# First experts' scores spread through a table in DRAM, groups routed two ahead, zeros written in the first layer

## The reference, cut to what matters

```
logits = x @ gate_w.T;  probs = softmax(logits);  topk_w = top_k(probs, 4) / its sum
scores = topk_w spread over 16 columns (0 for the experts not chosen)      # [tokens, 16]
g, u = x @ w1[e], x @ w3[e]                                                # 16 experts, 64 hidden features
out  = sum over e of ( silu(g) * u  @ w2[e] ) * scores[:, e]
```

## Time and profile before

| | us |
|---|---|
| median of three runs | 3887.02 |
| the profiled execution | 3887.59 |
| its span (first to last instruction) | 3885.8 |
| of which layer 0's experts, from its first load to the next stage | 674.9 to 1111.3 |

### The profile page before, as it was taken

One profiled execution on the slowest core, in us unless ns is written; L12 is line 12 of the kernel. 1 busy time (PEld: TensorE's weight loads), 2 busy tenths in 40 slices (PEclk: granted clock), 3 DMA queues, 4 the chain that ended last, 5 costly groups with the idle time before them and its releaser, 6 DMA issues. The chain is left out here.

```text
span 3885.8 us, 78038 instructions
## 1 busy us (share of the span) xinstructions
PE 2962.6 (76%) x23501; PEld 1869.2 (48%) x23501; DVE 3009.3 (77%) x12214; ACT 2259.2 (58%) x4496; POOL 1882.8 (48%) x2125
## 2 busy tenths in 40 slices
PE   3777776899979999699399967886777677677357
PEld 1222222444447777354277655554555555555245
DVE  6999998566667787343688867886999999999456
ACT  4999998333336666243266645664666666666230
POOL 5777776000013656577344452223236666666661
PEclk9999999999989999799699989998566766666585
DMA  2000000850000000153300000000001110000037
GB/s 76 5 5 5 5 5 19 374 250 1 1 14 14 27 28 27 46 142 114 97 15 15 15 13 1 2 2 12 12 25 50 33 31 7 5 5 4 1 101 228
DMA packets 161160, 177.79 MB, mean 46 GB/s; under 512 B 71906, under 2 KB 136324, under 8 KB 153323
## 3 DMA queue, kind: packets, MB, share of 16 engines
q1 hardware_dynamic: 128108, 140.65, 11.7%
q0 software_dynamic: 23424, 27.94, 2.1%
q10 hardware_dynamic: 9216, 4.20, 0.4%
HBM read 80.48 MB, written 113.61 MB: 50 GB/s over the span
## 5 line engine op out<-in xcount | busy, mean ns | idle before, releaser
L405 PE MATMUL PS<-IDENT,a_T 128*77 128x128 f32 (+1 forms) x3584 | 588.3, 302 | 157.9 <-ACT a_Pr L556 138.6
L1062 ACT ACTIVATE l_H<-l_H 128x2048 f32<-128x2048 f32 (+2 forms) x256 | 597.4, 2711 | 2.9 <-POOL l_H L1114 2.7
L405 PEld LDWEIGHTS PS<-IDENT,a_T 128*77 128x77 f32 (+1 forms) x3584 | 464.2, 164 | 243.3 <-ACT a_Pr L556 105.5
L1114 POOL TENSOR_TENSOR l_H<-l_feat,l_text 128x4096 f32<-128x4096 f32 x64 | 450.4, 7038 | 131.4 <-PE PS L1018 130.7
L1018 PE MATMUL PS<-l_H,l_wide 128*32 128x512 f32 (+1 forms) x2560 | 332.1, 594 | 165.2 <-ACT l_H L1062 165.2
L1136 DVE TENSOR_TENSOR l_H<-PS,l_text 128x2048 f32<-128x2048 f32 (+1 forms) x192 | 411.7, 2146 | 2.1 <-ACT l_text L1089 2.1
L558 ACT ACTIVATE a_Pr<-PS 77x512 f32<-77x512 f32 (+1 forms) x640 | 374.7, 587 | 60.5 <-PE PS L405 60.5
L422 PE MATMUL PS<-a_Pr,a_vaug 77*32 77x128 f32 (+1 forms) x7168 | 306.2, 316 | 23.4 <-ACT a_OT L597 15.8
L659 POOL TENSOR_TENSOR a_T<-a_mx,a_T 128x616 f32<-128x616 f32 x128 | 155.5, 1215 | 292.7 <-DVE a_mx L725 292.7
L2676 POOL DMA_INDIRECT expert_rows<-e3r_row,e3r_rows_at x256 | 253.5, 990 | 89.4 <-issue 74.7
L109 POOL TENSOR_TENSOR RSTD<-norm_tmp,MINUS_HALF 128x24 f32<-128x24 f32 x6 | 25.1, 4189 | 553.2 <-DVE norm_tmp L102 553.2
(11 more groups left out here) (382 smaller groups left out, 7871.6 us busy)
## 6 DMA issues: line engine op xcount, KB each, us to landing
pair_rows<-e_zero SPq DMA_DIRECT2D x35, 1024.0 KB, 25.3
expert_shares<-e_zero SPq DMA_DIRECT2D x16, 1024.0 KB, 25.7
e3c_four<-expert_shares SPq DMA_DIRECT2D x64, 256.0 KB, 3.7
e_xin<-pair_rows SPq DMA_DIRECT2D x39, 264.0 KB, 3.1
e_four<-pair_shares SPq DMA_DIRECT2D x16, 512.0 KB, 4.1
e_w<-in_L_ffn_blocks SPq DMA_DIRECT2D x39, 194.0 KB, 2.5
e3x_xin<-expert_rows SPq DMA_DIRECT2D x32, 200.0 KB
expert_rows<-e_zero SPq DMA_DIRECT2D x6, 1024.0 KB, 24.8
```

The source lines that it names most:

```text
L405: last = pe.transpose(PS[0:keys, 4 + g % 2, j * S:(j + 1) * S], T[:, u, c:c + keys], m.IDENT[:, :])
L1062: act.activation(cells, cells, ACT.Tanh).then_inc(q[f"tanh{part}"], 1)
L1114: pool.tensor_tensor(H[:, a, lo * S:hi * S].rearrange("p (t f) -> p t f", f=S), bcast(feat[:, a, :], 1, hi - lo), bcast(text[:, a, lo:hi], ...
```

## The change

It alters five things.

1. The pick product, its bf16 matrix, its load (`c_pick_pairs`, 288 KB) and cast, the split in three bf16 parts and their four transposes go. VectorE's `route_weights` ends with the fp32 scores; TensorE turns them with one fp32 transpose of 128x64 (`turn_scores`, pair 7, into bank 4), ScalarE copies 64x128 into `scT`.
2. SyncE writes `scT` in four transfers of 8 KB to a table in DRAM (16 experts x 512 tokens, one of two), waits for them, and reads the table back in two transfers of 1 MB: in each, every one of 64 partitions gets the 2 KB rows of the 8 experts that are first (or second) in their pair. The result, `wide` [128, 8 x 512] fp32, two of them, is what `hid` now multiplies with, from SBUF. The read waits for the last `hid` of the group that used the buffer before.
3. Groups are routed two ahead: `turn_y`, logits, the routing and `turn_scores` of step s are of group s+2 (yT in three buffers), `normalise_group` is of group s+3. The first group's products start after two routings and not one.
4. VectorE waits at pair 0 for both reads of its group.
5. The zeroed tile is made by GpSimd in `layer0_cross`' first block, and the 59 zeroing transfers are issued there, one a step after the load of `qm`; SyncE waits for all at that stage's end.

The diff, cut to its core:

```diff
@@ layer0_cross, SyncE's step
+                if i == 0:
+                    sp.wait_ge(m.s_zero, 1)
+                clear_part(sp, m, zero, i)
             run_written_out(sp, step, 0, 0)
+            sp.wait_ge(m.s_cleared, m.cleared)
@@ route_weights
-    dve.tensor_copy(parts[:, :, 0:E], sc).then_inc(q["hi"], 1)
-    dve.tensor_tensor(rest, sc, parts[:, :, 0:E], ALU.subtract).then_inc(q["rest1"], 1)
-    dve.tensor_copy(parts[:, :, E:2 * E], rest).then_inc(q["mid"], 1)
-    dve.tensor_tensor(rest, rest, parts[:, :, E:2 * E], ALU.subtract).then_inc(q["rest2"], 1)
-    dve.tensor_copy(parts[:, :, 2 * E:3 * E], rest).then_inc(q["parts"], 1)
@@ layer0_experts
+        @block.sync
+        def _(sp):
+            for i in range(NG):
+                u = i % 2
+                table = m.scores[u * E:(u + 1) * E, :]
+                sp.wait_ge(q["scTs"], i + 1)
+                if i >= 2:
+                    sp.wait_ge(q[f"wide{u}"], i // 2 * 32)
+                for g in range(G):
+                    sp.dma_start(table[:, g * S:(g + 1) * S], scT[g * E:(g + 1) * E, u, :]).then_inc(q[f"kept{u}"], 16)
+                sp.wait_ge(q[f"kept{u}"], (i // 2 + 1) * (G * 16))
+                if i >= 2:
+                    sp.wait_ge(q["hid"], nth_part(i, NP - 1, NP, 2 * NP))
+                for half in range(2):
+                    sp.dma_start(wide[64 * half:64 * half + 64, u, :].rearrange("f (p n) -> f p n", n=N),
+                                 table.rearrange("(p h) n -> h p n", h=2)[half].partition_broadcast(64)) \
+                        .then_inc(q[f"wide{u}"], 16)
@@ TensorE
-                if p == 0:
-                    pe.wait_ge(q["partsTs"], q.nth("partsTs", i))
-                if past_part(i, p, NP, 1):
-                    pe.wait_ge(q["hid"], nth_part(i, p, NP, 1))
-                pe.matmul(PS[:, 4, :], pick[:, p * 128:(p + 1) * 128], r.partsT[:, u, :],
-                          start=True, stop=True).then_inc(q["up"], 1)
+            def turn_scores(i):
+                pe.wait_ge(q["prob"], i + 1)
+                if i >= 1:
+                    pe.wait_ge(q["scTs"], i)
+                pe.transpose(PS[0:G * E, 4, 0:S], r.sc[:, i % 2, :], m.IDENT[:, :]).then_inc(q["scT"], 1)
-            run_written_out(pe, step, 1, 1, NG)
+            for s in range(-2, NG + 1):
@@ VectorE
+                        if p == 0:
+                            dve.wait_ge(q[f"wide{u}"], (s // 2 + 1) * 32)
-                        dve.tensor_tensor(hid[:, v, :], gu[:, v, :], PS[:, 4, :], ALU.mult).then_inc(q["hid"], 1)
+                        dve.tensor_tensor(hid[:, v, :], gu[:, v, :], wide[:, u, p * N:(p + 1) * N], ALU.mult) \
+                            .then_inc(q["hid"], 1)
```

More of the change, by code:

```diff
@@ L943, in layer0_cross @@
         one = sb("one", [S, 1])
+        zero = sb("zero", [128, 2048])
         q = Signals(ctx, nc, "l0", [
@@ L1227 @@
 N = G * S
-ROWS = 72
 PAD = 8
@@ L1344, in front_tensor @@
[L1344 to L1372, removed]
@@ L1418, in layer0_experts @@
         total = sb("total", [D, 2, N])
-        zero = sb("zero", [128, 2048])
-        q = Signals(ctx, nc, "e0", ROUTE_SIGNALS + ["prep", "up", "silu", "gu", "hid", "down"])
+        q = Signals(ctx, nc, "e0", ROUTE_SIGNALS + ["up", "silu", "gu", "hid", "down", "scT", "scTs", "kept0", "kept1",
+                                                    "wide0", "wide1"])
         PS = m.PS
@@ L1451, in _, with turn_y, logits @@
         @block.tensor
         def _(pe):
-            turn_y, logits, turn_parts = front_tensor(pe, m, q, y, yT, gate, r, E)
-            def up(i, u, p):
+            def turn_y(i):
+                pe.wait_ge(q["y"], i + 1)
+                if i >= 1:
+                    pe.wait_ge(q["yT"], i)
+                for g in range(G):
+                    last = pe.transpose(PS[:, 6, g * S:(g + 1) * S], y[:, i % 2, g * D:(g + 1) * D], m.IDENT[:, :])
+                last.then_inc(q["yTps"], 1)
+            def logits(i):
+                pe.wait_ge(q["yT"], i + 1)
+                if i >= 3:
+                    pe.wait_ge(q["x"], i - 2)
+                for g in range(G):
+                    last = pe.matmul(PS[:, 7, g * E:(g + 1) * E], yT[:, i % 3, g * S:(g + 1) * S], gate[:, :],
+                                     start=True, stop=True)
+                last.then_inc(q["logits"], 1)
@@ L1472, in down @@
             def down(i, p):
                 pe.wait_ge(q["hid"], nth_part(i, p, NP))
-                if p == 0:
-                    if past(i, 1):
-                        pe.wait_ge(q["total"], q.nth("total", i, 1))
-                last = pe.matmul(PS[:, 5, :], w2[:, p, :], hid[:, p % 2, :], start=(p == 0), stop=(p == NP - 1))
-                last.then_inc(q["down"], 1)
-            def turn_total(i, u):
-                pe.wait_ge(q["total"], q.nth("total", i))
-                pe.wait_ge(q["lt"], q.nth("lt", i, -1, NG))
+                if p == 0 and i >= 1:
+                    pe.wait_ge(q["total"], i)
@@ L1483, in turn_total @@
+                pe.matmul(PS[:, 5, :], w2[:, p, :], hid[:, p % 2, :], start=(p == 0), stop=(p == NP - 1)) \
+                    .then_inc(q["down"], 1)
+            def turn_total(i):
+                pe.wait_ge(q["total"], i + 1)
+                pe.wait_ge(q["lt"], min(i + 2, NG - 1) + 1)
                 for g in range(G):
-                    last = pe.transpose(PS[:, 7, g * D:(g + 1) * D], total[:, u, g * S:(g + 1) * S], m.IDENT[:, :])
+                    last = pe.transpose(PS[:, 7, g * D:(g + 1) * D], total[:, i % 2, g * S:(g + 1) * S], m.IDENT[:, :])
@@ L1562, in _ @@
             norm_gpsimd_rest(pool, m)
-            pool.memset(zero[:, :], 0.0).then_inc(m.s_zero, 1)
-        @block.sync
-        def _(sp):
-            clear_rows(sp, m, zero)
 PAIR = 2
@@ L2377, with clear_part @@
 PLACES = B * S * CHOSEN
-def clear_rows(sp, m, zero):
+def clear_part(sp, m, zero, i):
     width = zero.shape[1]
-    sp.wait_ge(m.s_zero, 1)
-    n = 0
     for table in (m.pair_rows, m.rows, m.shares):
         flat = table.rearrange("(p a) d -> p (a d)", p=128)
-        for c in range(0, flat.shape[1], width):
+        parts = -(-flat.shape[1] // width)
+        if i < parts:
+            c = i * width
             part = min(width, flat.shape[1] - c)
             sp.dma_start(flat[:, c:c + part], zero[:, 0:part]).then_inc(m.s_cleared, 16)
-            n += 16
-    m.cleared = n
-    sp.wait_ge(m.s_cleared, n)
+            m.cleared += 16
+            return
+        i -= parts
 def make_router(nc, m, t, ctx, wfT, row, own, rank, hid):
@@ L3245, in laid_out @@
     out["c_width_features"] = width.T
-    row, pair = np.arange(72), np.arange(8)
-    half = 2 * pair[None, :, None] + (f // 64)[None, None, :]
-    out["c_pick_pairs"] = ((row[:, None, None] % 16 == half) & (row[:, None, None] < 48)).astype(np.float32)
     for dh in (8, 16):
```

154 lines of the change are left out of this document (68 added, 86 removed).

## The result

The changed kernel takes **3852.59 us**, the median of four runs (3851.86 to 3856.70), against 3888.80 (3886.40 to 3891.39, four runs) for the kernel before: a ratio of 0.9909, 95% interval 0.9892 to 0.9926, so 0.9% faster, 36 us by the medians. The forecast was 3857.

A forecast was written before the change was run, and what follows sets the result against it. TensorE's own time and its waits were taken to bound layer 0's experts. From 3887.6 us, 40.7 less for the groups and 10.9 more for the opening gave 3857.8, as a median 3857; range 3845 to 3877.

The forecast's parts named there:

- The group: Layer 0's experts: a routed group falls from 25.82 to 23.4 us; over all groups 40.7 us less.
- The stall: TensorE's wait at pair 6 or 7 for ScalarE's two table loads: grows from 0.40 to 0.75 us a group.
- the turn of the scores: One fp32 transpose replaces four bf16 ones on TensorE: 0.17 us for 0.25, 0.08 gained a group.
- Rival B: Ordinary pairs become bound by the chain to hid: 1 us a group, 16 in all, 3873 us; chance 0.14.
- The opening: Start of the experts' stage: first hid 9.9 us late, plus 1.0 for half clock, costing 10.9 us.
- the data time T: Time for a group's 2.1 MB table read, scaled from broadcast row length: 13.1 us at 160 GB/s.
- The clock: TensorE products at half clock after idling in the opening: 1.0 us added, bounds 0 to 3.
- The reads in the steady state: Table reads after group 0 stay hidden up to T about 20 us: no wait, 7 us of cover.
- Rival A: The table reads bound each group, from below 105 GB/s; at 79 GB/s 3985 us; chance 0.10.
- The zeros: Zeroing transfers moved into layer 0's attention: no effect on its time.
- Rival C: The zeroing slows layer 0's attention by 1%: 3863 us; at 5% 3888; chance 0.06.
- D: The stall before the turn at pair 7 stays: 13.6 us back, 3871 us; chance 0.05.

The follow-up runs named there:

- the run without tables: Changed kernel with ScalarE computing 1 + 0.05 x in place of the experts' exponential, so no activation table loads; ratio 0.9892 to the kernel before.
- short rows: Changed kernel with eight reads of 256 KB a group, in pieces of 512 B in place of 2 KB; 3986.6 us beside 4022.9 for the kernel before.
- the routing one ahead: Changed kernel with groups routed one ahead, not two, so reads are issued in the step that uses them; 4220.1 us beside 4038 for the kernel before.
- the transfer with two outermost entries: Kernel with the turn moved, reading a re-laid table in one 2 MB transfer whose outermost dimension is the two halves; 4177.6 us, ratio 1.0741.
- the turn moved: Changed kernel with the turn back of a group's output moved from pair 2 to pair 5, its X addition a step later; 3850.59 us, ratio 0.9892.
- the run of their own: Kernel before with only the 59 zeroing transfers moved to layer 0's attention; ratio 0.9980.
- the split kept: Changed kernel with VectorE's five splitting instructions put back before the turn of the scores, their output unused; ratio 0.9942 to the kernel before.
- the long rows: Kernel with the turn moved, its table re-laid in 16 KB pieces and read by two transfers of 64 partitions; 3854.5 us beside 3892.8 for the kernel before.

## Why the prediction was right, step by step

**The group.** Forecast 23.4, measured 23.21. The pick products' 1.74 and the 0.97 before the turn came as worked out. The stall is 0.63 in the place of 0.75, but the load of w2, for which I had added 0.1, now lengthens the product behind it by 0.10: together 0.33 more than before, where I had 0.35. Its cause was right: the run without tables takes it all away, and the run with a transpose put into it takes 0.45. The term that was mis-sized is the turn of the scores. It holds TensorE 0.11 us (747.30 to 747.41), not 0.17, and the w1 product behind it takes 0.86, where it took 0.92 behind the four transposes (746.32 to 747.24): 0.20 gained and not 0.08. So 25.82 - 1.74 - 0.97 - 0.20 + 0.33 = 23.24. Over the 13 pitches from turn to turn the group gives 2.2 us more than forecast, the first group 0.4 less, the last two 0.1 more: this is the 1.9 between -40.7 and -42.6.

**hid from SBUF and the ordinary pairs.** Nothing was forecast and nothing came: hid takes 0.692 us in the place of 0.686, and without the tables TensorE is busy through all of a group. Rival B, an idle time before down in ordinary pairs, did not come about.

**The block before.** -2.1 forecast, -1.75 measured. I had the first y 0.35 us behind GpSimd's last instruction; it follows the barrier, 1.0 behind it (GpSimd ends at 679.01, y starts at 680.03).

**The opening.** +9.9 forecast for the first hid, +7.7 measured from the stage's first load (24.07 to 31.73); of the 2.2 between them 1.8 is the data time T, 11.3 us (693.5 to 704.8) where I had 13.1. That the value was near is luck, for the step of the reasoning that gave it was wrong: I had scaled the rate by the row's length, and short rows showed that the length hardly matters (213 against 202 GB/s for a quarter of it). Whatever held the broadcasts of the earlier trace rows at 27 to 79 GB/s, it was not that their rows had only 512 B; pieces of 308 B were not run.

That two transfers of 64 partitions are slower than one of 128 was the rule of the Trainium skill ("SBUF — State Buffer", "Door 1: The DMA port swizzle" and the section behind it on two DMAs for both halves), which the prediction weighed and set aside. The traces agree with it as far as they go: 213 GB/s in two halves, where the page has 196 for one transfer of 1 MiB, against 323 in one transfer across both (of half as many different rows); and its T of 10.7 was nearer to 11.3 than mine. Why the halves are slower is not shown here.

**The clock.** +1.0 forecast (0 to 3), 0 in the profiled execution: the down product at 705.61 ran at full clock after 3.0 us without work. With the turn moved it cost 1.7 in the opening, with the short rows 2.2. The bound was right to be there, and that the changed kernel paid nothing is luck.

**The reads in the steady state.** Forecast 7 us of cover. The read of a group is issued at 727.44, lands after at most 12.1, and its first hid starts at 750.68: 11 us of cover. Rival A failed on the rate, 213 GB/s and not under 105 (its own sum, 78 and 24 us on top of 3887, makes 3989 and not 3985); what it would have cost is seen with the routing one ahead, and the transfer with two outermost entries is a case of it, at 54 GB/s: 327 us more on the stage than with the turn moved alone.

**The zeros.** Nothing forecast, and the run of their own shows nothing. Rival C falls. D falls with the turn's missing idle time.

## What to carry to other kernels

Instructions on an engine that isn't the bound cost their full time where they end a chain that the bound engine waits for: the split's 0.97 us a group was as dear as more than half of the pick products' 1.74. A wait that one engine imposes whatever the others do (here two table loads) can be filled with work of the waiting engine that has no date, as the turn back of the output. Moving such work costs nothing in the steady state, but look at the opening and the end too: there the clock of TensorE took back 2.2 of the 5.7 us in the execution profiled here. When a transfer is made fewer and larger, look at its DMA share: the number of entries in its outermost dimension decided here how many of the engines took part.

## What was not expected of the hardware

- One transfer of 2 MB with 2 entries outermost moved 54 GB/s at a DMA share of 0.12; the same bytes in two transfers with 64 outermost 214 GB/s at 1.01, and one transfer with 128 partitions outermost (half as many different rows) 323 GB/s at 1.03.
- Broadcast reads from DRAM into 64 partitions went at 202 GB/s in pieces of 512 B, 213 in pieces of 2 KB, 214 in pieces of 16 KB.
- TensorE's granted clock at the first down product of the stage, after a stretch without work: at full after 3.0 and 2.0 us in two executions of the changed kernel, after 2.7 without tables and 2.3 with the split kept; at half after 2.3 with the turn moved, 3.2 with the long rows and 4.5 with the short ones. Behind the 11.9 us of the routing one ahead it was at half for 4.7 us. The length of the stretch alone doesn't tell it; what does stays open.
- Some chips took 4023 to 4038 us for the kernel that takes 3887 to 3893 on others, nearly all of it in layers 1 and 3; the first two stages were alike within 2 us. Why stays open.
